# Layer 0's probabilities turned by VectorE and ordered through DRAM, and the norm sums of layer 1 moved to the next round

## The chip, the core and the metric

The kernel runs on one core of one Trainium2 chip. The metric is the device time of one execution in microseconds (us). Three executions of the kernel before took 3765.32, 3766.14 and 3766.64 us; the median is 3766.14.

## What is computed

x is 64 graphs of 256 nodes with 512 features, adj their 256x256 adjacency masks. Two pre-normed layers follow one another, each added to x. All is float32. Cut to what matters:

```python
h = jnp.maximum(_layernorm(x), 0.0)                       # layer 0
q, k, v = (split_heads(h @ W) for W in (Wq, Wk, Wv))      # 4 heads of 64
sim = jnp.einsum('bhid,bhjd->bhij', q, k) * scale
attn = jax.nn.softmax(jnp.where(adj, sim, neg), axis=-1)
x = x + merge_heads(jnp.einsum('bhij,bhjd->bhid', attn, v)) @ Wo + bo

h = jnp.maximum(_layernorm(x), 0.0)                       # layer 1, 8 heads of 64
m = h @ map_w.T + map_b
n = m_heads / jnp.maximum(norm(m_heads), COS_EPS)
cos_adj = (n @ n.T * ~adj) > THRESHOLD
q, k = m @ q_w.T + q_b, m @ k_w.T + k_b
p = softmax(where(adj, NEG, q @ k.T / sqrt(dk))) * keep
a = cos_adj * p
sem = h @ gcn_map_w.T + gcn_map_b
out = relu((a @ sem) @ gcn_W.T / (a.sum(-1) + 1.0))
x = x + out
```

## The kernel before

**Rounds.** One round handles two graphs at once: layer 1's attention of graph a (steps written as pairs, `("score", 2)`) and, of the next graph n = a + 1, layer 0 and the products of layer 1 that need only its features (steps written as strings, `"qk0"`). `rounds` (L271) writes the first round (n only, with weights still being folded), a loop over 62 rounds, one more round after the loop, and a last round (a only).

**Orders.** Each engine works through a hand-written list of steps in every round: TENSOR (L51), SCALAR (L58), VECTOR (L64), POOL (L73, GpSimd) and SYNC (L78, SyncE, which issues all DMAs of the rounds). An engine never leaves its order; a step waits at its head for semaphores of the others. So a wait holds up all that stands behind it on that engine.

**Precision.** Most products are made in three passes of fp32r (high x high, high x low, low x high; PASSES, L16). For that ScalarE writes the rounded high part of a result from PSUM to SBUF and VectorE then writes the low part, the difference. A product that needs this operand waits for both: PSUM, ScalarE, VectorE, TensorE. Matmuls with a transposed or a probability operand are plain float32.

**PSUM.** Banks 0 and 1 hold scores of layer 1 (a pair of heads), 2 and 3 cosines, 4 the values. All other products share banks 5, 6 and 7 in turn, in the order in which TENSOR lists them (`bank_of`, L86); `empty` (L912) makes TensorE wait until the bank's last user has been read out. When the list changes, so do the banks.

**Layer 0 of graph n.** ht0a, ht0b (L1026): eight TensorE transposes of h. qk0 to qk3 (L1031): q and k of two pairs of heads, 12 matmuls each. s0/s1 and s2/s3 (L1044): scores of a pair of heads, 12 matmuls of 64 rows with the two heads side by side. VectorE adds the mask and takes the row maximum (L811), ScalarE makes the exponential and the row sum (L629), VectorE the reciprocal ("sum", L818), GpSimd the scaling (L517). pt0 to pt3 (L1052): four TensorE transposes of 128x128 for each head, which ScalarE copies from PSUM to `ptm` (L636). av (L1057): probabilities times v0, 16 matmuls. wo0, wo1 (L1063); VectorE adds them to x_mid (L824) and takes the statistics, GpSimd the power for 1/deviation (`rstd_of`, L456), VectorE normalises ("norm1", L675). ht1a, ht1b: eight transposes, from which gT comes.

**Layer 1.** m0 to m3 (L1067) make m; ScalarE writes it to `m32` (L642), GpSimd its squares to `msq` (L524). `m32` and `msq` are the two halves of `ptm`: the buffer holds probabilities first and m afterwards. "ss" (L1085) sums the squares by head (16 small matmuls), VectorE clamps them (L846), "pow" on GpSimd makes the factor 1/norm (L547), "rt" (L1092) turns the factors, VectorE copies them in two parts (L848, L850), "bc0" and "bc1" (L1098) spread them over the partitions, VectorE multiplies m by them (L853). "unit" 0 and 1 then split the normed m into high and low: ScalarE L645, GpSimd L502 (semaphores nhigh_done and nlow_done). For each of four pairs of heads p: score p (L1006), cos p (L1011, which needs unit p // 2), on VectorE score_a/b (mask, L760), on ScalarE exp_a/b (L605), on VectorE cos_a/b (threshold and product, L771).

**How layer 1 turns its weights.** The 256x256 matrix of each head is to be transposed for the product with v. It is laid out in `att` in 32x32 blocks, so that one VectorE instruction ("flip", L779, 128x512) turns all blocks of a head in place. SyncE then writes the pair's 512 KB to `scratch` in DRAM ("spill", L390) and reads it back in four parts of 128 KB, one for each block column, into `uT` ("shift", L397), which puts the blocks in order. value p (L1015) uses it. `by_quarter` (L961) makes the score and cos products write their columns in this block order.

**The rest.** "back" p turns the values back, VectorE and GpSimd add them to x_res (L794, L510). "factor" p: three small VectorE operations. "mid" (L489): GpSimd adds bo to x. "mask0" (L481) and "mask1" make the masks. SYNC also has x (load), adj, out (store) and move (x_mid to x_res).

## Time and profile before

| | |
|---|---|
| median of three executions | 3766.14 us |
| the profiled execution | 3767.53 us |
| its span, first to last instruction | 3765.7 us |
| mean granted TensorE clock | 0.994 |
| busy: TensorE | 3665.0 us, 97% |
| busy: VectorE | 2723.6 us, 72% |
| busy: ScalarE | 1695.4 us, 45% |
| busy: GpSimd | 1357.2 us, 36% |
| DMA moved | 381.35 MB, 101 GB/s |

Busy time is the time in which at least one instruction of the engine ran; the shares are of the span. The sixteen DMA engines together are counted as one share. In a timeline or a chain the ends of TensorE's blocks overlap, so what a block takes is read from the start of the next one. "L949" is a line of the kernel; one helper line serves several steps, and the operands tell which. The chain of waits starts at the last instruction and goes back to what released each one; "issue" in it is time in which the engine waited for nothing that the profile shows.

### The profile page before, as it was taken

How to read it: one execution, taken by the hardware profiler on the slowest of the kernel's cores; microseconds unless marked ns; L12 is line 12 of the kernel's file. 1: busy time of each engine (PE TensorE's matmuls, PEld its weight loads, DVE VectorE, ACT ScalarE, POOL GpSimd, SP SyncE). 2: the span in 40 equal slices, each digit the busy share in tenths (PEclk: the TensorE clock that was granted, in tenths of full speed). 3: DMA queues.
4: the chain of work that ended last, by engine and by line, in shares of the span. 5: the costliest groups of instructions: out<-in, count | busy, mean ns of one | idle time of the engine just before them, and what ended most of it. 6: DMA issues, size and time to landing. Idle time of an engine off the chain costs nothing.

```text
span 3765.7 us, 101867 instructions
## 1 busy us (share of the span) xinstructions
PE 3665.0 (97%) x31020; PEld 3224.1 (86%) x31020; DVE 2723.6 (72%) x9432; ACT 1695.4 (45%) x5075; POOL 1357.2 (36%) x2069
## 2 busy tenths in 40 slices
PE   8999999999999999999999999999999999999997
PEld 5888888888888888888888888888888888888885
DVE  3777777777777777777777777777777777777765
ACT  2444444444444444444444444444444444444443
POOL 2333433433433333334334334334333333343331
PEclk9999999999999999999999999999999999999998
DMA  2223323233233233333232332322332333332323
GB/s 94 91 96 106 99 99 107 94 108 102 96 112 102 96 109 100 102 104 104 97 107 98 100 107 94 109 102 96 112 102 96 108 100 102 103 104 98 107 86 107
DMA packets 250601, 381.35 MB, mean 101 GB/s; under 512 B 41328, under 2 KB 173968, under 8 KB 250576
## 3 DMA queue, kind: packets, MB, share of 16 engines
q1 hardware_dynamic: 250304, 380.73, 30.4%
q0 software_dynamic: 272, 0.30, 0.0%
q8 instruction: 13, 0.21, 0.0%
q14 instruction: 12, 0.10, 0.0%
HBM read 179.61 MB, written 167.77 MB: 92 GB/s over the span
## 4 chain that ended last, share of the span: by engine, by line
PE 89%; DVE 5%; issue 4%; DMA 1%; DVEq 1%; POOL 0%; ACT 0%; SPq 0%; POOLq 0%; ACTq 0%
PE bank L949 35%; PE bank L957 19%; PE bank L973 14%; PE bank L981 8%; PE bank L942 7%; PE bank L1090 3%; DVE h L675 1%; DVE x_mid L824 1%; PE bank L1024 1%; PE bank L1102 1%; DVE rel L794 1%; PE bank L898 1%; PE bank L1096 1%; DVE mv L669 0%; DVE rec L785 0%
## 5 line engine op out<-in xcount | busy, mean ns | idle before, releaser
L605 ACT ACTIVATE att<-att,nmax 128x256 f32<-128x256 f32 x1024 | 508.1, 501 | 83.5 <-DVE nmax L760 83.5
L771 DVE SCALAR_TENSOR_TENSOR att<-bank,att 128x256 f32<-128x256 f32 x1024 | 404.9, 421 | 33.0 <-ACT att L605 18.3
L949 PE MATMUL bank<-gT,w_k 128*128 128x256 f32 x3072 | 417.2, 285 | 0.5 <-DVE k L841 0.5
L949 PE MATMUL bank<-gT,w_q 128*128 128x256 f32 x3072 | 414.6, 284 | 2.7 <-DVE w_k L698 1.4
L949 PEld LDWEIGHTS bank<-gT,w_map 128*128 128x128 f32 x3072 | 370.7, 188 | 34.3 <-issue 25.8
L949 PE MATMUL bank<-gT,w_map 128*128 128x256 f32 x3072 | 396.9, 285 | 1.1 <-DVE gT L801 1.1
L949 PE MATMUL bank<-hT,w_qkv 128*128 128x256 f32 x3072 | 392.6, 284 | 4.4 <-DVE hT L801 4.4
L949 PEld LDWEIGHTS bank<-gT,w_k 128*128 128x128 f32 x3072 | 386.7, 189 | 8.2 <-DVE k L841 0.7
L957 PE MATMUL bank<-w_v,gT 128*128 128x512 f32 x1536 | 385.2, 399 | 0.0
L949 PEld LDWEIGHTS bank<-hT,w_qkv 128*128 128x128 f32 x3072 | 373.2, 189 | 13.6 <-DVE w_o L689 4.8
L949 PEld LDWEIGHTS bank<-gT,w_q 128*128 128x128 f32 x3072 | 380.3, 189 | 3.7 <-DVE w_k L698 2.2
L760 DVE CUSTOM_DVE_ANT_0 att<-bank,mask 128x256 f32<-128x256 f32 x1024 | 378.8, 417 | 1.5 <-PE bank L973 1.5
L629 ACT ACTIVATE prob<-prob,nmax 128x256 f32<-128x256 f32 x512 | 255.2, 500 | 248.8 <-DVE nmax L811 248.8
L524 POOL TENSOR_TENSOR ptm<-ptm 128x256 f32<-128x256 f32 x256 | 157.5, 615 | 549.1 <-ACT ptm L642 546.9
L517 POOL TENSOR_SCALAR prob<-prob,rsum 128x256 f32<-128x256 f32 x512 | 242.4, 486 | 294.7 <-DVE rsum L818 294.7
L502 POOL TENSOR_TENSOR nrm<-ptm,nrm 128x512 fp32r<-128x512 f32 x128 | 166.1, 1298 | 486.0 <-ACT nrm L645 486.0
L779 DVE STREAM_TRANSPOSE att<-att 128x512 f32<-128x512 f32 x512 | 339.6, 692 | 0.0
L957 PEld LDWEIGHTS bank<-w_v,gT 128*128 128x128 f32 x1536 | 279.2, 188 | 58.6
L460 POOL TENSOR_SCALAR var_e<-mv 128x2 f32<-128x2 f32 x128 | 24.7, 193 | 755.7 <-DVE mv L669 750.1
L981 PE MATMUL bank<-uT,v 128*64 128x256 f32 x2048 | 276.2, 390 | 13.5 <-DMA uT<-scratch 13.5
L587 ACT ACTIVATE q<-bank,bias_q 128x256 fp32r<-128x256 f32 x128 | 60.8, 475 | 490.8 <-PE bank L949 490.8
L510 POOL TENSOR_TENSOR x_res<-x_res,rel 128x256 f32<-128x256 f32 x256 | 203.1, 793 | 198.9 <-DVE rel L794 198.9
(136 smaller groups left out, 7042.9 us busy)
## 6 DMA issues: line engine op xcount, KB each, us to landing
scratch<-att SPq DMA_DIRECT2D x256, 512.0 KB, 2.6
uT<-scratch SPq DMA_DIRECT2D x1024, 128.0 KB, 3.0
x_in<-x SPq DMA_DIRECT2D x64, 512.0 KB, 3.7
x_res<-x_mid SPq DMA_DIRECT2D x64, 512.0 KB, 2.9
out<-x_res SPq DMA_DIRECT2D x64, 512.0 KB, 2.8
adj<-adj SPq DMA_DIRECT2D x64, 64.0 KB, 1.9
att<-gcn_map SPq DMA_DIRECT2D x1, 1024.0 KB, 10.9
att<-map_rows SPq DMA_DIRECT2D x1, 1024.0 KB, 6.4
```

The costliest lines, as they stand in the source:

```text
L510: g.tensor_tensor(part, part, rel[:, :, :], ALU.add).then_inc(res_added, 1)
L517: last = g.tensor_scalar(prob0[:, hd, c, :], prob0[:, hd, c, :], rsum0[:, hd, c:c + 1], 0.0, ALU.mult, ALU.add)
L605: s_.activation(e_sl, e_sl, ACT.Exp, bias=nmax1[:, p, c, e:e + 1], scale=-1.0, accum_out=esum1[:, p, c, e:e + 1]).then_inc(exp1_done, 1)
L629: last = s_.activation(prob0[:, hd, c, :], prob0[:, hd, c, :], ACT.Exp, bias=nmax0[:, hd, c:c + 1], scale=-1.0, accum_out=esum0[:, hd, c:c ...
L760: v_.tensor_tensor_reduce(out=att[:, p % 2, :, e, c, :, :].rearrange("p b j f -> p b (j f)"), in0=in_blocks(score_bank[e][:, c * N:c * N + ...
L771: v_.scalar_tensor_tensor(e_sl, in_blocks(gram_bank[e][:, c * N:c * N + N]), COS_THRESHOLD, e_sl, ALU.is_gt, ALU.mult, accum_out=usum1[:, ...
L779: v_.transpose(blocks, blocks).then_inc(flipped, 1)
L942: last = t_.transpose(dst[:, b * 128:b * 128 + 128], src_of(outer, c), ident[:, :])
L949: last = t_.matmul(dst, w(ws, k)[:, t * 128:t * 128 + 128], rhs[:, rs, k, :], start=(k == 0 and i == 0), stop=(k == KT - 1 and i == 2))
L957: last = t_.matmul(dst, lhs[:, ls, k, c * 128:c * 128 + 128], w(ws, k), start=(k == 0 and i == 0), stop=(k == chunks - 1 and i == 2))
L973: last[e] = t_.matmul(order(banks[e][:, c * N:c * N + N], False), left[r, ls, c * 128:c * 128 + 128], order(right[r, rs, :], True), start= ...
L981: last = t_.matmul(dst[64 * e:64 * e + 64, :].rearrange("p (c r f) -> p c r f", c=C, f=32), v[:, jc, (hd0 + e) * DH:(hd0 + e + 1) * DH], r ...
```

## The change

1. **Turning.** `prob0` gets the block layout of `att`. The s products write in that order (`by_quarter`), mask0 is made in it (two GpSimd instructions of one row half each in place of one), and the operations of VectorE, ScalarE and GpSimd on the probabilities address it so. The steps pt0 to pt3 go, on TensorE and on ScalarE. In their place VectorE turns each head in place (turn0 to turn3, one 128x512 instruction each, after GpSimd's scaling), and SyncE writes each pair of heads to a new DRAM buffer `scratch0` (send0, send1) and reads it back in four parts into `ptm` (fetch0, fetch1). av waits for both pairs.
2. **Norm factors.** ss, pow, rt, bc0 and bc1 of a graph are no longer done at the end of the round that made m, but near the start of the next one, as ("ss", 0), ("pow", 0), ("rt", 0), ("bc", 0), ("bc", 1). So `m32` and `msq` live into that round, and the first fetch waits for nlow_done of both unit steps.
3. **Orders.** All five lists are written anew; with them the banks change. Among SyncE's steps the load of x stands between spill 3 and shift 3.

```diff
@@ the lists @@
     TENSOR = [
-        ("score", 0), "ht0a", "ht0b", ("k", 2), "qk0", "qk1", ("q", 2), ("cos", 0), "s0", "s1", ("score", 1), "qk2", "qk3",
-        ("vv", 0), "pt0", ("score", 2), ("cos", 1), "s2", "s3", "v0", "pt1", ("vv", 1), "pt2", "pt3", ("cos", 2), "av",
-        ("value", 0), ("cos", 3), "wo0", "wo1", ("k", 3), ("back", 0), ("q", 3), ("value", 1), "ht1a", "ht1b", ("back", 1),
-        ("score", 3), "m0", "m1", "m2", ("value", 2), "m3", "q0", ("back", 2), "ss", "q1", "k0", ("value", 3), "rt", "k1",
-        "bc0", "bc1", ("back", 3)
+        ("score", 0), "ht0a", "ht0b", ("ss", 0), "qk0", "qk1", ("rt", 0), "s0", "s1", "qk2", ("bc", 0), "qk3", ("bc", 1),
+        ("score", 1), "s2", "s3", ("cos", 0), ("k", 2), ("vv", 0), ("cos", 1), ("q", 2), ("vv", 1), "v0", ("cos", 2),
+        ("score", 2), ("value", 0), "av", ("q", 3), ("back", 0), "wo0", "wo1", ("k", 3), ("value", 1), ("score", 3),
+        ("back", 1), "ht1a", "ht1b", ("cos", 3), "m0", "q0", "m1", ("value", 2), "q1", "k0", "m2", ("back", 2), "k1",
+        ("value", 3), "m3", ("back", 3)
     ]
     SCALAR = [
+        "ht0a", "ht0b", ("exp_a", 0), "qk0", "qk1", ("exp_b", 0), "exp0", "qk2", ("unit", 0), "qk3", "exp1", "exp2", "exp3",
+        ("unit", 1), ("k", 2), ("q", 2), ("exp_a", 1), ("exp_b", 1), ("exp_a", 2), ("value", 0), ("exp_b", 2), "av", ("q", 3),
+        ("k", 3), ("value", 1), "ht1a", "ht1b", ("exp_a", 3), ("exp_b", 3), "m0", "q0", "m1", "q1", "k0", ("value", 2), "m2",
+        ("value", 3), "k1", "m3"
     ]
     VECTOR = [
+        ("score_a", 0), ("score_b", 0), "ht0a", "ht0b", ("ss", 0), "qk0", "qk1", ("rt", 0), "s0", "s1", ("bc", 0), "qk2",
+        "sum0", "qk3", ("bc", 1), "sum1", "turn0", "s2", "s3", "turn1", ("cos_a", 0), "sum2", ("cos_b", 0), "sum3",
+        ("flip_a", 0), ("flip_b", 0), ("k", 2), "turn2", "turn3", ("vv", 0), ("score_a", 1), ("q", 2), ("score_b", 1),
+        ("cos_a", 1), ("vv", 1), ("cos_b", 1), ("flip_a", 1), "v0", ("flip_b", 1), ("score_a", 2), ("score_b", 2),
+        ("cos_a", 2), ("factor", 0), ("factor", 1), ("flip_a", 2), "av", ("back", 0), ("cos_b", 2), ("q", 3), "wo0", "wo1",
+        ("flip_b", 2), ("k", 3), "norm1", ("score_a", 3), ("score_b", 3), "ht1a", "ht1b", ("factor", 2), ("cos_a", 3),
+        ("cos_b", 3), ("flip_a", 3), ("flip_b", 3), ("back", 1), ("factor", 3), "q0", "q1", ("back", 2), "stats0", "k0",
+        "norm0", "k1", ("back", 3)
     ]
     POOL = [
+        ("pow", 0), "mask0", "mid", ("unit", 0), "sum0", "sum1", "sum2", ("unit", 1), "sum3", "rstd1", ("back", 0), "mask1",
+        ("back", 1), "m0", "m1", "rstd0", ("back", 2), "m2", "m3", ("back", 3)
     ]
     SYNC = [
+        "send0", ("spill", 0), "fetch0", "send1", ("shift", 0), "fetch1", ("spill", 1), ("shift", 1), ("spill", 2),
+        ("shift", 2), ("spill", 3), "x", ("shift", 3), "adj", ("out", 0), "move"
     ]
@@ layout @@
-        prob0 = sb("prob0", [128, H0, C, N])
+        prob0 = sb("prob0", [128, PAIRS0, 4, 2, C, C, 32])
+        pT_blocks = [ptm[:, 2 * t:2 * t + 2, :].rearrange("p e n -> p (e n)").rearrange("p (r e c j f) -> p r e c j f", e=2, c=C, j=C, f=32)
+                     for t in range(PAIRS0)]
@@ SyncE @@
+                    elif kind in ("send0", "send1"):
+                        t = int(kind[4])
+                        sp.wait_ge(pturned, H0 * n + 2 * t + 2)
+                        if a is not None:
+                            sp.wait_ge(pT_in[t], 64 * n)
+                        sp.dma_start(scratch0[t, :, :, :, :], prob0[:, t, :, :, :, :, :].rearrange("p b e c j f -> p b e (c j f)")).then_inc(sent0[t], 16)
+                    elif kind in ("fetch0", "fetch1"):
+                        t = int(kind[5])
+                        sp.wait_ge(sent0[t], 16 * n + 32)
+                        sp.wait_ge(nlow_done, 2 * n + 2)
+                        for cols in range(4):
+                            sp.dma_start(pT_blocks[t][32 * cols:32 * cols + 32, :, :, :, :, :].rearrange("p r e c j f -> p r (e c j f)"),
+                                         scratch0[t, :, cols, :, :].rearrange("(r p) e x -> p r (e x)", p=32)).then_inc(pT_in[t], 16)
@@ VectorE @@
+                    elif kind in ("turn0", "turn1", "turn2", "turn3"):
+                        hd = int(kind[4])
+                        dve.wait_ge(prob0_done, H0 * n + hd + 1)
+                        blocks = prob0[:, hd // 2, :, hd % 2, :, :, :].rearrange("p b c j f -> p b (c j f)")
+                        v_.transpose(blocks, blocks).then_inc(pturned, 1)
@@ TensorE @@
-                        for last in head_products(pair_banks, qkm[:, :, t, :], qkm[:, :, 2 + t, :]):
+                        for last in head_products(pair_banks, qkm[:, :, t, :], qkm[:, :, 2 + t, :], by_quarter):
-                    elif kind[:2] == "pt":
-                        hd = int(kind[2])
-                        pe.wait_ge(prob0_done, H0 * n + hd + 1)
-                        empty(a, n, kind)
-                        transposes(full, lambda jc, c: prob0[:, hd, c, jc * 128:jc * 128 + 128]).then_inc(product_full, 1)
                     elif kind == "av":
-                        pe.wait_ge(pT_ready, H0 * n + H0)
+                        for t in range(PAIRS0):
+                            pe.wait_ge(pT_in[t], 64 * n + 64)
...
```

The steps ss, pow, rt and bc keep their instructions; only their place in the lists and their semaphores change. In the diff, waits of one engine are followed by a semaphore increment for bookkeeping, left out here.

## Rows read from the trace of the kernel before

**Rows 1.** The page: span, busy time by engine; costliest groups (busy us, mean ns); DMA issues (KB, us to landing)

```profile
span 3765.7 us, 101867 instructions
...
PE 3665.0 (97%) x31020; PEld 3224.1 (86%) x31020; DVE 2723.6 (72%) x9432; ACT 1695.4 (45%) x5075; POOL 1357.2 (36%) x2069
...
L779 DVE STREAM_TRANSPOSE att<-att 128x512 f32<-128x512 f32 x512 | 339.6, 692 | 0.0
...
uT<-scratch SPq DMA_DIRECT2D x1024, 128.0 KB, 3.0
```

**Rows 2.** TensorE's waits over the whole run: total us, times, longest

```profile
PE bank L942 <- DVE h L675: 61.1, 64, 8.4
```

**Rows 3.** Windows of a steady round and the last: length, busy us by engine, clock, DMA share, GB/s

```profile
1933.40:1990.60 57.20, 56.36 (x485) 49.86 (x484) 42.33 (x148) 26.25 (x79) 21.07 (x32) 1.00 0.30 102
...
3711.80:3765.70 53.90, 28.98 (x209) 20.98 (x208) 24.43 (x98) 12.79 (x42) 6.18 (x7) 0.76 0.32 108
```

**Rows 4.** Chain of waits, longest pieces: the same block, first and last of 62

```profile
106.07 5.67 PE bank L949 x48
...
3593.24 5.67 PE bank L949 x48
```

**Rows 5.** Chain of waits in one steady round: start us, us, what

```profile
1933.46 0.92 PE bank L973 x12
...
1941.07 2.34 PE bank L973 x36
...
1958.27 0.87 PE bank L942 x8
...
1971.51 0.12 issue
...
1982.56 1.68 PE bank L1090 x16
```

**Rows 6.** Timeline of TensorE: start us, us, line, operation

```profile
1906.47 3.06 PE L957 MATMUL bank<-w_o,oT 128*128 128x512 f32 x12
1909.37 1.58 PE L949 MATMUL bank<-gT,w_k 128*128 128x256 f32 x12
...
1930.96 0.38 PE L1096 MATMUL bank<-ident,rn 128*8 128x128 f32 x2
...
1936.65 3.00 PE L949 MATMUL bank<-hT,w_qkv 128*128 128x256 f32 x24
```

**Rows 7.** Timeline of VectorE: start us, us, line, operation

```profile
1911.00 0.41 DVE L669 BATCH_NORM_AGGREGATE mv<-stats 128x2 f32<-128x6 f32 x2
...
1927.12 0.17 DVE L846 TENSOR_SCALAR ssq<-bank 128x16 f32<-128x16 f32 x1 [0.91 <-PE bank L1090]
...
1931.83 0.41 DVE L850 TENSOR_TENSOR rnT<-bank,rnT 8x256 fp32r<-8x256 f32 x1
...
1940.11 0.43 DVE L805 TENSOR_TENSOR qkm<-bank,qkm 128x256 fp32r<-128x256 f32 x1 [1.00 <-ACT qkm L621]
```

**Rows 8.** Timeline of GpSimd: start us, us, line, operation

```profile
1911.98 0.71 POOL L463 TENSOR_TENSOR rstd<-var_e,minus_half 128x2 f32<-128x2 f32 x1 [0.18 <-POOL var_e L460]
...
1927.37 2.90 POOL L547 TENSOR_TENSOR rn<-ssq,minus_half 128x16 f32<-128x16 f32 x1 [1.23 <-DVE ssq L846]
```

**Rows 9.** Timeline of SyncE: a spill and its fetch undisturbed, then one beside the load of x

```profile
1912.35 0.34 SPq L396 DMA_DIRECT2D scratch<-att  x1
1915.16 1.73 SPq L404 DMA_DIRECT2D uT<-scratch  x4
...
1951.77 0.35 SPq L396 DMA_DIRECT2D scratch<-att  x1
...
1954.83 1.75 SPq L404 DMA_DIRECT2D uT<-scratch  x4
```

**Rows 10.** Windows: DMA share while one spill, then one fetch of 512 KB moves

```profile
1912.40:1915.20 2.80, 1.96 (x17) 1.30 (x16) 2.72 (x8) 1.23 (x3) 1.00 (x2) 1.00 0.46 187
1916.10:1919.50 3.40, 3.40 (x34) 3.26 (x33) 3.40 (x15) 2.19 (x9) 0.44 (x1) 1.00 0.58 154
```

More of the change, by code:

```diff
@@ L231, in gnn_two_layers @@
         high_done = count("high_done")
-        pT_ready = count("pT_ready")
+        pturned = count("pturned")
+        sent0 = [count(f"sent0_{t}") for t in range(PAIRS0)]
+        pT_in = [count(f"pT_in{t}") for t in range(PAIRS0)]
         m_ready = count("m_ready")
@@ L927, in empty @@
                 m = G - 1 if n is None else n - back
[L928 to L931 removed]
+                if user in MAPPED:
                     if a is not None or not back:
@@ L995, in body @@
                         full = bank[bank_of[s]]
-                    if kind in ("q", "k", "vv"):
+                    if kind == "ss":
+                        pe.wait_ge(msq_done, KT * a + KT)
+                        empty(a, n, s)
+                        for t in range(KT):
+                            for c in range(C):
+                                last = t_.matmul(full[:, c * H1 + 2 * t:c * H1 + 2 * t + 2], msq[:, t, c * 128:c * 128 + 128], half_of[:, :], start=True, stop=True)
+                        last.then_inc(later_full, 1)
+                    elif kind == "rt":
+                        pe.wait_ge(rn_done, a + 1)
+                        empty(a, n, s)
+                        for c in range(C):
+                            last = t_.transpose(full[0:H1, c * 128:c * 128 + 128], rn[:, c * H1:c * H1 + H1], ident[:, :])
+                        last.then_inc(later_full, 1)
+                    elif kind == "bc":
+                        pe.wait_ge(later_done, later_out_of_psum(a, ("rt", 0)))
+                        empty(a, n, s)
+                        for t in range(2):
+                            last = t_.matmul(full[:, t * N:t * N + N], pick[:, 2 * p + t, :], rnT[:, :], start=True, stop=True)
+                        last.then_inc(later_full, 1)
+                    elif kind in ("q", "k", "vv"):
                         pe.wait_ge(product_done, out_of_psum(a, "ht1b"))
```

104 lines of the change are left out of this document (40 added, 64 removed), and 4 rows, old and new, of the table SCALAR.

## The prediction

> **What bounds the kernel now.** I read the busy shares first: TensorE is busy 97% of the span, VectorE 72%, ScalarE 45%, GpSimd 36% [rows 1]. The reader is to see that one engine is nearly full. Then the waits: TensorE's one wait of size in the rounds is at the transposes of the second layernorm, 61.1 us in 64 times, all others being small or in the first and last rounds [rows 2]. The windows say the same of one round: TensorE idle 0.84 us of 57.2, at a granted clock of 1.00, VectorE busy 42.3 [rows 3]. The period comes from a block that the chain of waits shows once a round: (3593.24 - 106.07) / 61 = 57.17 us [rows 4]. So a steady round is 56.33 us of TensorE's work and 0.84 us of waiting, and there are 62 such in the loop and one after it. The last round is 53.9 us in which TensorE is busy 29.0, so there the chain of one graph sets the time [rows 3]. The profiled execution took 3767.5 us (span 3765.7), 1.4 above the median of the runs, 3766.1; my differences are added to the median.
>
> **What the change takes from TensorE.** Sixteen transposes of probabilities a round go. Eight take 0.87 us in the chain [rows 5], so sixteen take 1.75. The blocks of score, cos and s products pay for each uninterrupted run of them: a single one costs 0.92 and three in a row 2.34 [rows 5], which is 0.71 each and 0.2 per run. The old order has six runs and the new one seven, so 0.2 comes back. The reordered reading (by quarters) of the s products costs nothing: the score and cos blocks in the run of 2.34 already read so. ss, rt and bc are moved, not removed; each graph pays them once. New work: 56.33 - 1.75 + 0.20 = 54.78 us. Break-even is therefore 57.17 - 54.78 = 2.39 us of waits a round, where there were 0.84.
>
> A rule speaks against the change. The Trainium skill, VectorE: DVE Perf Modes, section Rules for kernel authors, says to use TensorE for a 128x128 transpose where PSUM can take the result, and that VectorE's transpose is the fastest only inside a bank of 32. By it the change would give up the right engine and buy a trip through DRAM; the rows give TensorE's side of the trade, 1.55 us a round before waits, and no row here shows the trip for layer 0.
>
> **What it puts on others.** VectorE gains four turns of a 128x512 tile, 0.65 each back to back (0.69 alone [rows 1]), 2.6 us, which makes 44.9 of 57: not the bound. ScalarE loses four evictions, GpSimd's mask becomes two instructions; neither is near full. DMA moves two more spills and two more fetches of 512 KB. One spill holds the engines 0.46 x 2.80 = 1.3 us, one fetch 0.58 x 3.40 = 2.0 [rows 10], so 6.6 us a round on a share of 0.30 (17 us) [rows 3]: about 0.42.
>
> **The new order, walked through.** t = 0 is the start of score 0.
> - Start: score, ht0, ss end at 0.92 + 0.87 + 1.68 = 3.5 [rows 5]; qk0 and qk1 follow, 2.84, to 6.3; rt could come and s0 at 6.45. But s0 needs the last eviction of qk1: in the trace qk0 starts at 1936.65 and VectorE ends the second copy at 1940.11 + 0.43, 3.89 later [rows 6, 7], and TensorE starts 0.12 after [rows 5]. Before, q2 and cos0 filled this; now only rt does. s0 starts at 7.5: **a wait of 1.05**. rt has its own wait, which lies inside: ssq is read after ht0b, at 3.9, GpSimd's power starts 0.25 later and takes 2.90 [rows 7, 8], so 7.1; it costs nothing while qk1's eviction is later.
> - qk2 then waits until rt is out of its bank (rt start to end of the second copy: 1931.83 + 0.41 - 1930.96 = 1.28 [rows 6, 7], so 8.4, plus 0.12) against 8.4 by work: 0.1 to 0.15; s2 waits about 0.1 for qk3. **0.2** together. cos0 needs bc0 (TensorE 10.2), VectorE's multiplication (11.1), unit 0 on ScalarE (11.7) and on GpSimd (13.05); TensorE gets there at 13.6. Behind the power wait on GpSimd stand mask0 (ready near 7.9, wanted at 8.6) and mid (wanted 27 us later): hidden, with 0.7 to spare for the mask.
> - The round trip. GpSimd scales head 0 only after unit 0, to 13.95; from there VectorE works almost without a break: turn0 to 14.65, s2 and s3 (0.7 each) to 16.05, turn1 16.7, cos 0 and both flips to 19.7, k2 20.1, turn2 20.75. turn3 waits for GpSimd, which does sum2, unit 1 and sum3 one after another to 20.7 (0.95, 1.3, 0.95), and ends at 21.45. SyncE issues in order: a spill is followed by its fetch 2.81 later (1912.35 to 1915.16), or 3.06 beside another transfer (1951.77 to 1954.83); the fourth part of a fetch is issued 1.3 into its 1.73 and lands 3.0 after that [rows 1, 9]. send1 goes out at 22.1, since fetch0 (which waits for unit1) fills the queue till then; 3.0 + 1.3 + 3.0 bring the second pair at 29.4, up to 30.3 with contention. TensorE, after value 0, wants it at 29.5. **0.3** taken (ends 0 and 0.8). shift 0, which now stands behind send1, lands at 27.5; value 0 wants it at 28.5. For this part TensorE does 21.7 us of work, so VectorE and the trip hide under it.
> - wo0 waits for VectorE's copy of av behind two factor steps and a flip, m0 for gT's behind four score steps: **0.2** together.
> - Layernorm of layer 1. Before, wo starts at 1906.47 and the mean and variance end at 1911.41, 4.94 later [rows 6, 7]; the power ends 1.28 after [rows 7, 8]; h needs 1.0 more. k3, back0, q3, value 1 stood between wo and ht1; now k3, value 1, score 3, back 1, 3.7 us in place of 4.25. score 3 waits for VectorE's copy of k3, behind the statistics and a flip: at 2.90 (wo, 1906.47 to 1909.37 [rows 6]) + 3.2 after wo's start; then ht1 waits a little for h. VectorE on its part drops a back and a factor step ahead of norm1. **0.85**, as much as the 0.84 before.
> - value 2 (data 0.7 early) and value 3 (0.1 to 0.4 early, with x's load now between spill 3 and shift 3): nothing, and this is where x's move can cost. The next ht0 finds h 0.5 early.
>
> Sum of waits: 1.05 + 0.2 + 0.3 + 0.2 + 0.85 = 2.6. Round: 54.78 + 2.6 = 57.4, 0.2 longer than 57.17. Over 63 rounds +13 us. The first round loses ss (1.68 [rows 5]), rt and bc (about 3 us with the wait for the power; its probabilities' trip is covered by the folding of weights that precedes av); the last one gets them with nothing beside them: score and ss 2.6, power 3.15, rt 1.3, bc0 with its multiplication and the unit steps 3 bring cos 0 at 10, where it stood at 6 behind score 0, k2 and q2; waits for later transfers hide part of the 4. I take -3 and +3, with ends -5 and +8 for their sum. Against the profiled execution's own time that is 3767.5 + 13 = 3780.5, against the median **3766.1 + 13 = 3779 us.** The waits I hold to 2.0 and 3.6, so rounds from 56.8 to 58.4.
>
> **Rivals.**
> - **A, the gates close early (faster).** My five waits are read from old neighbours. If the lead that VectorE gets while TensorE waits for s0 carries through, the trip, wo0, m0 and qk2 cost nothing and score 3 half: 1.05 + 0.45 = 1.5 to 2.0, a round of 56.5, 3766.1 - 0.65 x 63 = 3725. For: many gates meet within 0.1 to 0.3 in my walk. Against: s0's wait follows from two rows and has no cover.
> - **B, transfers collide (slower).** Between 19.9 and 29.4 spill 0, fetch0, send1, shift 0 and fetch1 need 2 x 1.3 + 3 x 2.0 = 8.6 us of the DMA engines [rows 10], nine tenths of that stretch. If each landing slips by 0.5, send1 and fetch1 bring av 1.0 later, and value 2 and value 3, past their slack, 0.3: 58.7 a round, 3766.1 + 1.5 x 63 = 3861; a third of it gives 3800. It decides where the second pair lands more than 0.3 after TensorE wants it at 29.5. For: 3.06 in place of 2.81 beside one other transfer [rows 9]. Against: that is a quarter of a microsecond only, and the share stays under 1. The Trainium skill, DMA: Bandwidth & Descriptors, section Latency and other measured facts, gives HBM's latency as 0.2 us on average and 2 at high load; by it B would be the case if such a stretch counts as high load, which no row here shows.
> - **C, all is hidden (faster).** Waits stay 0.84: 55.6 a round, 3665. Against: the s0 wait alone forbids it, unless the eviction of qk1 overlaps in a way that the rows don't show.
>
> **Numbers.** My own case (57.0 to 57.9 a round, 3755 to 3812) gets 0.43, of it 0.13 within 0.2% of 3766, 0.28 slower, 0.02 faster; A 0.29 (of it 0.02 within); C 0.07; B 0.21. 0.2%, 7.5 us, is about what a measurement of this kernel can tell from none. Faster 0.36, same 0.15, slower 0.49. My case's own range is 3755 to 3812; for 8 in 10, with A down to 3712 and the nearer half of B, I give 3712 to 3835.
>
> **What would show it.** Right: the block of 48 or its successor returns every 57.4 us; TensorE waits before the s products on VectorE's qkm copy (1.05 x 63 = 66 us) and before the k,q products on VectorE's k (about 45); prob transposes are gone. A: the period near 56.5, waits of TensorE of 1.8 or less. B: TensorE waits for a fetch from scratch0 by over 1 us a round, and transfers land later than 3.0. Wrong altogether: a wait on GpSimd's power or its sums, or VectorE as releaser at many small places.

## The result, and the profile after

The changed kernel takes 3973.58 us in the median (3973.0 to 3979.24), the kernel before 3766.24 beside it: ratio 1.0554, 95% interval 1.0536 to 1.0573. It is slower, by 207 us, far outside the range of the prediction (3712 to 3835).

The page of the changed kernel: span, busy times, and DMA issues with KB and us to landing.

```profile
span 3977.4 us, 100973 instructions
...
PE 3686.2 (93%) x29996; PEld 3148.7 (79%) x29996; DVE 2890.9 (73%) x9688; ACT 1578.3 (40%) x4819; POOL 1353.4 (34%) x2133
...
scratch<-prob SPq DMA_DIRECT2D x128, 512.0 KB, 3.1
ptm<-scratch SPq DMA_DIRECT2D x512, 128.0 KB, 3.2
```

Against [rows 1] TensorE has 1,024 instructions fewer, the transposes, and yet is busy 21 us longer. Its share fell from 97% to 93%: something else now holds it up. TensorE's waits of the changed kernel (total us, times, longest):

```profile
PE bank L1012 <- DMA ptm<-scratch: 87.8, 62, 2.0
PE bank L1004 <- DVE k L768: 47.1, 63, 0.8
PE bank L1038 <- POOL rn L577: 39.6, 64, 3.3
PE bank L1012 <- DMA uT<-scratch: 36.7, 74, 4.7
PE bank L973 <- DVE h L701: 28.4, 64, 8.4
```

Where there was one wait of size in the rounds [rows 2] there are five, and the greatest ends with a transfer from scratch0: av waits 1.4 us in every round of the loop. L768 is score 3 behind k3, L577 is rt behind GpSimd's power. The windows of one round, of two stretches of its round trip, and of the last round:

```profile
2022.82:2082.92 60.10, 56.33 (x467) 48.43 (x467) 44.90 (x152) 24.42 (x75) 21.00 (x33) 1.00 0.42 132
2062.50:2066.50 4.00, 4.00 (x30) 3.68 (x29) 3.97 (x17) 2.17 (x8) 0.00 (x0) 1.00 0.95 294
2066.50:2071.20 4.70, 3.18 (x37) 2.25 (x35) 3.59 (x16) 1.85 (x8) 0.00 (x0) 1.00 0.95 249
3919.70:3979.00 59.30, 34.21 (x218) 25.50 (x218) 25.31 (x99) 12.85 (x42) 8.94 (x8) 0.72 0.29 99
```

VectorE's 44.9 and the DMA share of 0.42 over a round are what was forecast against [rows 3]. But in the 8.7 us that end with av the DMA engines are busy 95% of the time. The same stretch in SyncE's timeline, and then in the chain of waits:

```profile
2056.88 0.35 SPq L401 DMA_DIRECT2D scratch<-prob  x1
2059.50 0.34 SPq L422 DMA_DIRECT2D scratch<-att  x1
2060.22 1.92 SPq L410 DMA_DIRECT2D ptm<-scratch  x4
2062.53 0.34 SPq L401 DMA_DIRECT2D scratch<-prob  x1
2063.15 2.09 SPq L430 DMA_DIRECT2D uT<-scratch  x4
2066.59 1.73 SPq L410 DMA_DIRECT2D ptm<-scratch  x4
```

```profile
2062.53 3.90 DMA scratch<-prob
...
2067.88 3.27 DMA ptm<-scratch
...
2071.48 1.95 PE bank L1012 x16
```

The second send (2062.53) takes 3.90 us to land where a lone spill and its fetch lay 2.81 apart [rows 9]; after it the fetch takes 1.3 to issue and 3.27 more. The chain now passes through this trip in every round: its shares are TensorE 29%, DMA 23%, issue 16%, VectorE 13%. Of the 23% only 11 are the trip (scratch<-prob 6, ptm<-scratch 5); 9 are the store and the move of x, which the chain reaches through GpSimd's "mid". But GpSimd stands idle after mid, as its timeline shows, and VectorE's under it:

```profile
2051.58 1.28 POOL L531 TENSOR_TENSOR nrm<-ptm,nrm 128x512 fp32r<-128x512 f32 x1 [1.08 <-ACT nrm L671]
```

```profile
2053.94 0.71 DVE L814 STREAM_TRANSPOSE prob<-prob 128x512 f32<-128x512 f32 x1 [0.71 <-POOL prob L547]
```

So mid is not what holds up the round. Unit 0 waits 1.08 us for its high part from ScalarE, which waits for VectorE's product behind bc0, and bc0 stands behind s0, s1 and qk2; head 0 is scaled only after unit 0, and turn0 waits 0.71 for that. The moved norm steps thus stand on the way from s0 to av. What they cost there no run shows, as none moves unit 0 alone.

**The granted clock.** It is 1.00 in the round above, but not in every round. In 15 of the 62 rounds of the loop it falls to 0.50, the lower of its two levels, for about 3.4 us. The fall comes within 0.5 us of av's start, after the two waits at value 0 and av. One such place, in two windows and TensorE's timeline:

```profile
1946.00:1949.60 3.60, 1.80 (x20) 1.02 (x19) 2.97 (x17) 2.14 (x8) 0.00 (x0) 1.00 0.97 276
1949.60:1953.00 3.40, 3.38 (x16) 1.90 (x16) 1.13 (x5) 0.20 (x2) 0.00 (x0) 0.50 0.34 95
```

```profile
1949.62 3.59 PE L1012 MATMUL bank<-ptm,v 128*64 128x256 f32 x16 [1.41 <-DMA ptm<-scratch]
```

av takes 3.5 us there in place of 1.9. A round with such a fall takes 61.9 us in the mean, one without 60.2. The kernel before has none in its loop.

**Where the 211.7 us between the two profiled spans went.** The norm sums ("ss") return once a round, so their starts measure it: 161.32 and, 61 rounds later, 3857.04, which is 60.58 a round, against 57.17 before. 62 rounds by 3.41 are +211. Some 3.0 of the 3.41 are longer rounds at full clock, 0.4 is the fallen clock (15 times 1.7 us). From the starts of score 0, the first round gives 5.0 back, the round after the loop takes 63.4 in both, and the last is 4.9 longer (58.8 against 53.9 [rows 3]). So everything is in the rounds of the loop, and the experiments are about those.

### The profile page after: what moved, and what is told of

It reads as the page before. It is cut to its first block, busy times and chain, and to the rows that moved or that the text cites. A ratio compares the mean times of both kernels' runs of the same rounds, so it can differ in the third digit from the quotient of the medians.

```text
span 3977.4 us, 100973 instructions
## 1 busy us (share of the span) xinstructions
PE 3686.2 (93%) x29996; PEld 3148.7 (79%) x29996; DVE 2890.9 (73%) x9688; ACT 1578.3 (40%) x4819; POOL 1353.4 (34%) x2133
## 4 chain that ended last, share of the span: by engine, by line
PE 29%; DMA 23%; issue 16%; DVE 13%; POOL 9%; SPq 6%; ACT 2%; DVEq 1%; POOLq 0%; ACTq 0%
PE bank L980 16%; DMA scratch<-prob 6%; PE bank L1012 5%; DMA ptm<-scratch 5%; PE bank L988 5%; SPq L410 5%; DMA x_res<-x_mid 5%; DMA out<-x_res 4%; POOL prob L547 2%; DVE h L701 2%; POOL x_mid L528 2%; DMA uT<-scratch 2%; DVE att L821 1%; DVE att L807 1%; DMA scratch<-att 1%
## 5 line engine op out<-in xcount | busy, mean ns | idle before, releaser
L980 PE MATMUL bank<-gT,w_map 128*128 128x256 f32 x3072 | 418.3, 285 | 12.9 <-DVE k L884 6.5
L980 PE MATMUL bank<-gT,w_q 128*128 128x256 f32 x3072 | 425.7, 288 | 1.4 <-DVE w_k L724 1.4
L980 PEld LDWEIGHTS bank<-gT,w_map 128*128 128x128 f32 x3072 | 379.8, 188 | 53.8 <-DVE k L884 34.7
L980 PE MATMUL bank<-hT,w_qkv 128*128 128x256 f32 x3072 | 413.5, 287 | 4.3 <-DVE hT L843 4.1
L807 DVE SCALAR_TENSOR_TENSOR att<-bank,att 128x256 f32<-128x256 f32 x1024 | 383.2, 416 | 3.4 <-PE bank L1004 3.2
L1004 PE MATMUL bank<-k,q 64*128 64x256 f32 x3072 | 245.6, 292 | 47.1 <-DVE k L768 47.1
L1004 PEld LDWEIGHTS bank<-k,q 64*128 64x128 f32 x3072 | 199.8, 186 | 95.7 <-issue 85.3
L847 DVE TENSOR_TENSOR qkm<-bank,qkm 128x256 fp32r<-128x256 f32 x256 | 108.1, 422 | 219.0 <-ACT qkm L651 219.0
L1004 PE MATMUL bank<-nrm 64*128 64x256 f32 x3072 | 247.2, 292 | 2.3 <-DVE att L807 1.6
```

The source lines that it names most:

```text
L807: v_.scalar_tensor_tensor(e_sl, in_blocks(gram_bank[e][:, c * N:c * N + N]), COS_THRESHOLD, e_sl, ALU.is_gt, ALU.mult, accum_out=usum1[:, ...
L847: v_.tensor_tensor(qkm[:, 1, 2 * w + t, :], full[:, 0:N], qkm[:, 0, 2 * w + t, :].bitcast(F32), ALU.subtract).then_inc(product_done, 1)
L980: last = t_.matmul(dst, w(ws, k)[:, t * 128:t * 128 + 128], rhs[:, rs, k, :], start=(k == 0 and i == 0), stop=(k == KT - 1 and i == 2))
L1004: last[e] = t_.matmul(order(banks[e][:, c * N:c * N + N], False), left[r, ls, c * 128:c * 128 + 128], order(right[r, rs, :], True), start= ...
```

## The experiments

In all of them the kernel changed is the base, unless the text says otherwise. The periods are read from the starts of "ss", as above.

**1. The trip left out.** SyncE's sends and fetches go, and av reads prob0 turned in place, so the ordering of the 32x32 blocks is left out.

```diff
-        "send0", ("spill", 0), "fetch0", "send1", ("shift", 0), "fetch1", ("spill", 1), ("shift", 1), ("spill", 2),
+        ("spill", 0), ("shift", 0), ("spill", 1), ("shift", 1), ("spill", 2),
@@ av @@
-                            last = values(full[:, t * N:t * N + N], v0, 2 * t, lambda e, jc: pT_blocks[t][:, :, e, :, jc, :]...
+                            last = values(full[:, t * N:t * N + N], v0, 2 * t, lambda e, jc: prob0[:, t, :, e, :, jc, :]...
```

> The changed kernel without layer 0's trip through DRAM: send0, send1, fetch0 and fetch1 are left out, av multiplies the turned blocks where they stand, out of order (the ordering of the blocks between 32-row groups is left out). All lists else as in the changed kernel. Theory T (the path of the second pair of heads, from turn3 through SyncE and DRAM to av, sets the round of 60.1 us): TensorE's waits before av (1.4 us) and value 0 (0.4) go and the round falls to 57.7 to 58.2, so about 3974 - 63 x 2.2 = 3835 us (3820 to 3855). Theory N (the moved norm steps with their waits before rt and s0 set it): TensorE is late at av anyway, the round stays over 59, 3900 or more.

Measured: 3838.76 us, ratio 1.0189 (1.016 to 1.0219), 58.30 a round. TensorE's timeline of this kernel at value 0 and av:

```profile
2051.80 1.08 PE L1012 MATMUL bank<-uT,v 128*64 128x256 f32 x8
2052.72 1.90 PE L1012 MATMUL bank<-prob,v 128*64 128x256 f32 x16
```

No wait stands between them. So the trip costs 60.58 - 58.30 = 2.28 us a round, 135 us in all. No round of the loop has a fallen clock here, so 0.4 of the 2.28 is the clock and 1.9 the waits. But this kernel, which pays nothing for ordering the blocks, is still slower than before: the trip is not the whole loss.

**2. The trip with a quarter of the bytes,** as many instructions on the same queue.

```diff
+                        part = 128 if a is None else 64
+                        heads = 2 if a is None else 1
+                        sp.dma_start(scratch0[t, :, :, 0:heads, 0:part], ...
+                            rows = 4 if a is None else 1
+                            sp.dma_start(pT_blocks[t][32 * cols:32 * cols + 32, 0:rows, ...
```

> The changed kernel with the same sixteen-odd instructions of the trip on SyncE, but after the first round each send and fetch moves only a quarter of its bytes (a quarter of the probabilities is ordered, the rest of ptm is left as it was). T by contention (the transfers stretch each other: the second send lands after 3.9 us where a spill alone took 2.6): landings fall to under 2.6, the wait before av goes, 3835 to 3870. T by queue (SyncE's order and the fixed part of a transfer): the data still come 1 us or more too late, 3900 to 3950. Theory N: no change, 3960 or more.

Measured: 3846.98 us, ratio 1.0211 (1.0181 to 1.0241), 58.4 a round; no wait at av. Of the 2.28 all but 0.1 goes with the bytes, and not with the instructions or the semaphores of the trip; the clock does not fall in the loop here either. The page's landings of this kernel:

```profile
scratch<-prob SPq DMA_DIRECT2D x126, 128.0 KB, 2.2
ptm<-scratch SPq DMA_DIRECT2D x504, 32.0 KB, 2.1
```

**3. Is it the neighbours' bytes or its own?** Layer 1's first pair, whose spill and shift run among the four new transfers, moves a quarter of its bytes (the rest of that pair's matrix is left out); layer 0's trip is whole. (One more load ahead of the loop costs 5.5 us.)

```diff
+                        heads, part = (1, 64) if p == 0 else (2, 128)
+                            rows = 1 if p == 0 else 4
```

> The changed kernel with layer 0's trip whole, but layer 1's first spill and its fetch (pair 0) moving only a quarter of their bytes by the same number of instructions (three quarters of that pair's turned matrix is left out; one more copy in DRAM at the start, some 3 us). Theory C (transfers that overlap stretch each other): fetch0 and send1 have less beside them, send1 lands after 3.0 to 3.3 instead of 3.9, the wait before value 0 goes and the one before av shrinks: 3974 - 63 x 1.2 + 3 = 3900 (3880 to 3925). If the landing is long because of its own bytes and of fetch0 alone: over 3940.

Measured: 3946.01 us, ratio 1.0477 (1.0447 to 1.0508). TensorE's waits of this kernel:

```profile
PE bank L1017 <- DMA ptm<-scratch: 98.0, 62, 2.4
```

value 0 no longer waits (8.7 us in the whole run) and the landings of the trip fall to 3.0 in the median. But the second send still takes 3.7 in the mean, against 3.9, and av still waits 1.6. The loss of 135 us falls by 28 (33 without the extra load), a quarter. That is the second expectation (over 3940). Of the gain 0.37 us a round is a shorter way to av; much of the rest is the clock, which falls in 2 rounds of the loop and not in 15. So the larger part goes with the trip's own bytes.

**4 and 5. The order on the queue.** send1 went out 1.0 us after turn3, behind fetch0. First it goes ahead of fetch0; then GpSimd also scales head 3 before unit 1.

```diff
-        "send0", ("spill", 0), "fetch0", "send1", ("shift", 0), "fetch1", ("spill", 1), ("shift", 1), ("spill", 2),
+        "send0", ("spill", 0), "send1", "fetch0", ("shift", 0), "fetch1", ("spill", 1), ("shift", 1), ("spill", 2),
@@ and in the second @@
-        ("pow", 0), "mask0", "mid", ("unit", 0), "sum0", "sum1", "sum2", ("unit", 1), "sum3", "rstd1", ("back", 0), "mask1",
+        ("pow", 0), "mask0", "mid", ("unit", 0), "sum0", "sum1", "sum2", "sum3", ("unit", 1), "rstd1", ("back", 0), "mask1",
```

> The changed kernel with send1 ahead of fetch0 on SyncE. In the changed kernel send1 was issued 1.1 us after turn3, behind fetch0's four parts, and landed 3.9 us later with fetch0 moving beside it. Theory Q+C (both the place in the queue and the collision count): send1 goes out 0.8 us earlier with one transfer fewer beside it, lands after 2.7 to 3.2, the second pair is there 1 us earlier but shift 0 a little later: the round loses 0.7 to 1.3 us, 3974 - 63 x 1.0 = 3911 (3890 to 3930). If only the number of bytes counts, whatever their order (theory C): within 20 us of 3974.

> As the run before, and on GpSimd sum3 ahead of unit 1, so that turn3 need not wait for unit 1's 1.3 us (turn3 ends 0.5 us earlier, fetch0 starts later). Theory T (the second pair's path sets the round): a further 0.3 to 0.8 us a round, 3860 to 3890, and not below the 3839 of the kernel without a trip.

Measured: 4083.24 us, ratio 1.0841 (1.081 to 1.0873), and 4028.71, ratio 1.0697 (1.0666 to 1.0728). Both are slower than the changed kernel; both expectations missed. The landings of the first, its waits, and its window over the three fetches:

```profile
scratch<-prob SPq DMA_DIRECT2D x128, 512.0 KB, 2.8
ptm<-scratch SPq DMA_DIRECT2D x512, 128.0 KB, 3.7
```

```profile
PE bank L1012 <- DMA uT<-scratch: 101.0, 71, 5.2
PE bank L1012 <- DMA ptm<-scratch: 88.3, 62, 1.6
```

```profile
2050.00:2060.40 10.40, 7.50 (x65) 6.21 (x63) 9.17 (x40) 4.62 (x17) 0.00 (x0) 1.00 1.03 249
```

The send lands sooner (2.8 in the median) and the fetches later (3.7): three fetches now run together, on DMA engines that are full (1.03). send1 is issued 0.8 us earlier, but fetch1 now stands behind all of fetch0 and shift 0 and is issued when it was before; its last part takes 4.4 us to land instead of 3.3, so the pair comes 1.0 later and value 0 is late as well. With that the clock falls in 30 of the 62 rounds, in 13 of them for 6.8 us: of the 110 us that this kernel loses on the changed one, about 60 are longer rounds at full clock (61.18 against 60.22) and much of the rest is the clock. The second kernel is 54.5 us better than the first. Its turn3 ends 0.63 us earlier after s0, and av starts 0.63 earlier: lateness on this way comes out one to one at av.

**6 and 7. The wait before s0.** Two kernels fill it. In the first, k2 stands between qk1 and rt on all three engines; in the second, score 1 stands before s0, on TensorE alone, which moves no bank.

```diff
-        ("score", 0), "ht0a", "ht0b", ("ss", 0), "qk0", "qk1", ("rt", 0), "s0", "s1", ...
+        ("score", 0), "ht0a", "ht0b", ("ss", 0), "qk0", "qk1", ("k", 2), ("rt", 0), "s0", "s1", ...
@@ the second @@
-        ..., ("rt", 0), "s0", "s1", "qk2", ("bc", 0), "qk3", ("bc", 1), ("score", 1), "s2", "s3",
+        ..., ("rt", 0), ("score", 1), "s0", "s1", "qk2", ("bc", 0), "qk3", ("bc", 1), "s2", "s3",
```

> The changed kernel with the step (k, 2) moved on TensorE, ScalarE and VectorE from behind cos 0 to between qk1 and rt, where TensorE waits 0.6 for rt and then for s0. Theory N: the cover takes 0.9 to 1.2 us out of every round, 3974 - 63 x 1.0 = 3910. Theory T: the waits at the front vanish and come back before av, since turn3 is not earlier: within 15 us of 3974.

> The changed kernel with one step of TensorE's list moved: score 1, 0.92 us, stands before s0 instead of behind bc1, and fills the 1.2 us that s0 waits for the eviction of qk1; no bank changes, as scores have their own. Everything is computed. Theory S (the waits of a round add up): 0.75 less a round, 3974 - 47 = 3927 (3910 to 3945). Theory P (a chain through the probabilities, from s0 over VectorE, GpSimd and the DRAM trip to av, sets the period; the wait before s0 costs nothing of its own and av waits by whatever the order gains): s0 comes no earlier, up to 0.1 later, av's wait stays near 1.6 plus what the order saved, 3970 to 3985.

Measured: 4067.29 us, ratio 1.0796 (1.0764 to 1.0827), and 4016.57, ratio 1.0661 (1.0643 to 1.0679). The first missed both numbers: with k2 moved, the banks shift, and the s products come to wait for k2's eviction (L768, 107.0 us in 127 times), so s0 starts 9.23 after score 0 instead of 7.76. That lateness of 1.47 came out one to one: the time rose by 93.7 us, 1.49 a round. The second kernel has no such side effect. Its timeline at rt, score 1, s0, and at av, with that of the changed kernel under it:

```profile
2064.16 0.38 PE L1038 MATMUL bank<-ident,rn 128*8 128x128 f32 x2 [0.58 <-POOL rn L577]
2064.48 0.99 PE L1004 MATMUL bank<-k,q 64*128 64x256 f32 x12
2065.30 0.88 PE L1004 MATMUL bank<-qkm 64*128 64x256 f32 x12
...
2070.68 0.98 PE L1004 MATMUL bank<-qkm 64*128 64x256 f32 x12 [0.88 <-DVE qkm L847]
...
2089.42 0.87 PE L1012 MATMUL bank<-ptm,v 128*64 128x256 f32 x6 [1.45 <-DMA ptm<-scratch]
```

```profile
2046.74 0.38 PE L1038 MATMUL bank<-ident,rn 128*8 128x128 f32 x2 [0.58 <-POOL rn L577]
2047.28 0.98 PE L1004 MATMUL bank<-qkm 64*128 64x256 f32 x12 [0.16 <-issue]
...
2052.74 0.98 PE L1004 MATMUL bank<-qkm 64*128 64x256 f32 x12
...
2071.48 1.30 PE L1012 MATMUL bank<-ptm,v 128*64 128x256 f32 x10 [1.44 <-DMA ptm<-scratch]
```

From rt to s0 it is 1.14 instead of 0.54, and from s0 to av 24.12 against 24.20: the same. s2, its cover gone, stands where it stood after s0 (5.38 and 5.46) and now shows a wait of 0.88. The 0.6 us by which s0 is later is the round's (43 us in all, 0.7 a round; 0.5 in the rounds at full clock). The waits do not add up (that theory expected 3927); the path from s0 over the softmax, the turns and the trip to av keeps its length, and TensorE's filling inside it buys nothing. The rival's mechanism holds; its number (3970 to 3985) was too low, as it allowed s0 0.1 us of lateness and not 0.6.

The means over the rounds of the loop show the same for all kernels so far. They are from TensorE's starts, in us; the first three columns are of rounds without a fall of the clock:

| | ss to s0 | s0 to av | av to the next ss | rounds with a fall, of 62 |
|---|---|---|---|---|
| the changed kernel | 5.92 | 24.30 | 30.00 | 15 |
| 1, no trip | 5.93 | 22.18 | 30.22 | 0 |
| 2, a quarter of the bytes | 5.93 | 22.21 | 30.30 | 0 |
| 3, neighbour lighter | 5.93 | 23.93 | 29.99 | 2 |
| 4, send1 first | 5.92 | 25.27 | 29.99 | 30 |
| 5, and sum3 earlier | 5.92 | 24.76 | 29.99 | 34 |
| 6, k2 early | 7.40 | 24.32 | 29.99 | 11 |
| 7, score 1 as cover | 6.52 | 24.16 | 30.01 | 16 |

In the rounds with a fall it is av to ss that is longer: 31.6 in the changed kernel, 32.0 in kernel 4.

**8. The turning alone, its lists half new.** The norm steps go back to the end of their own round, the trip stays.

```diff
-        ("score", 0), "ht0a", "ht0b", ("ss", 0), "qk0", "qk1", ("rt", 0), "s0", "s1", "qk2", ("bc", 0), "qk3", ("bc", 1),
+        ("score", 0), "ht0a", "ht0b", "qk0", "qk1", "s0", "s1", "qk2", "qk3",
...
-        ("value", 3), "m3", ("back", 3)
+        ("value", 3), "rt", "k1", "bc0", "bc1", ("back", 3)
```

> The turning by VectorE and the trip alone: ss, pow, rt and bc are back at the end of the round that made m, in the order that the kernel before has there; the lists else as in the changed kernel. Theory N: the round falls to about 57.5, 3800 us or less. Theory T: the trip is as long as before, but its start, s0, comes 2 us earlier after the start of the round (5.7 where it was 7.8) because ss and rt no longer stand ahead of it, while TensorE's work before av shrinks by as much, so the wait before av stays 1 us or more; the rest gains from the front's waits: 58.5 to 59.5 a round, 3880 to 3930.

Measured: 4257.43 us, ratio 1.13 (1.1268 to 1.1333). A miss that decides little: the lists written for it made new waits of their own (hT 104.5 us, qkm 75.3, rel 53.9), the mean granted clock was 0.97, and the wait at av stayed, 88.3.

**9. The norm steps and lists alone.** TensorE keeps the sixteen transposes (between q2 and cos 2, as the new order has room), no turns, no trip.

```diff
-        ("score", 1), "s2", "s3", ("cos", 0), ("k", 2), ("vv", 0), ("cos", 1), ("q", 2), ("vv", 1), "v0", ("cos", 2),
+        ("score", 1), "s2", "s3", ("cos", 0), ("k", 2), ("vv", 0), ("cos", 1), ("q", 2), "pt0", ("vv", 1), "pt1", "v0",
+        "pt2", "pt3", ("cos", 2),
```

> The other part alone: the norm steps in the next round and the new lists, but layer 0's probabilities transposed by TensorE and copied by ScalarE as in the kernel before (pt0 behind q2, pt1 behind vv1, pt2 and pt3 behind v0). Theory N (the moved norm steps and the new lists cost by themselves): the kernel without a trip took 58.3 us a round; sixteen transposes add 1.75, so 60.0 a round, 3838.8 + 110 = 3949 us (3925 to 3965), that is as slow as the whole change. If the turning and the trip are the only loss: 3766 to 3800.

Measured: 3985.16 us, ratio 1.0581 (1.055 to 1.0612), beyond the expectation. TensorE's waits of this kernel and its busy time:

```profile
PE bank L984 <- DVE k L754: 39.3, 63, 0.6
PE bank L984 <- DVE qkm L825: 27.8, 62, 0.9
PE bank L1018 <- POOL rn L558: 24.0, 50, 3.3
```

```profile
PE 3796.2 (95%) x31020; PEld 3259.2 (82%) x31020; DVE 2753.9 (69%) x9432; ACT 1702.2 (43%) x5075; POOL 1346.6 (34%) x2069
```

It runs the instructions of before, 31,020 on TensorE, in 219 us more, of which the busy time takes 131. Some 20 of these are 14 rounds of the loop in which the granted clock falls to 0.50 for 3.4 us, here at qk0 and qk1, and which take 61.7 us in place of 60.2. For the rest, a matmul's busy time in the profile includes a tail during which the next one may already start (the blocks of the timelines overlap by some 0.1 us), and short waits hide in it. Block starts against block starts, one round each: qk0 and qk1 take 3.50 where two such blocks took 2.84 before, rt to s0 0.70 (rt's work is 0.14), score 0 1.09 for 0.92, and so on.

**10. The other corner: old lists, no transposes.** The lists of before; the four pt steps give way to four turns on VectorE, no trip.

```diff
-        ("vv", 0), "pt0", ("score", 2), ("cos", 1), "s2", "s3", "v0", "pt1", ("vv", 1), "pt2", "pt3", ("cos", 2), "av",
+        ("vv", 0), ("score", 2), ("cos", 1), "s2", "s3", "v0", ("vv", 1), ("cos", 2), "av",
@@ VectorE @@
-        "sum2", ("cos_a", 1), ("factor", 0), "v0", "sum3", ("cos_b", 1), ("flip_a", 1), ("flip_b", 1), ("score_a", 2),
+        "sum2", ("cos_a", 1), "turn1", ("factor", 0), "v0", "sum3", "turn2", ("cos_b", 1), "turn3", ("flip_a", 1), ...
```

> The lists of before with only this exchanged: the four transposing steps of layer 0 leave TensorE and ScalarE, VectorE turns the four heads, the norm steps stay at the end of their round. The order of the 32x32 blocks is left out (no DRAM trip; av reads prob0 turned in place), so layer 0's values are not the reference's. With the runs so far this completes a two-by-two: old or new lists, with or without the sixteen transposes. Theory N (moving the norm steps with the lists written for it costs about 3.4 us a round, and the transposes are worth their 1.75): round 57.17 - 1.75 = 55.4, 3655 us (3645 to 3685). Theory L (the new lists are not the loss by themselves; what the norms-only kernel paid came of transposes that no longer fitted in the new order): the old lists without transposes gain little since GpSimd and VectorE gates close, 3740 or more.

Measured: 3791.28 us, ratio 1.0067 (1.005 to 1.0084), 57.68 a round. Theory N's 3655 is off by 136; theory L's number (3740 or more) is met, though it spoke of a small gain and this is a small loss. The greatest wait of this kernel, and its timeline from cos 2 to cos 3:

```profile
PE bank L1004 <- DVE att L798: 100.9, 126, 1.0
```

```profile
2026.90 0.99 PE L1004 MATMUL bank<-nrm 64*128 64x256 f32 x12 [0.63 <-DVE att L798]
2027.82 1.95 PE L1012 MATMUL bank<-prob,v 128*64 128x256 f32 x16
2030.00 1.08 PE L1012 MATMUL bank<-uT,v 128*64 128x256 f32 x8 [0.23 <-DVE v L755]
2032.06 0.98 PE L1004 MATMUL bank<-nrm 64*128 64x256 f32 x12 [0.98 <-DVE att L798]
```

Sixteen transposes, 1.84 us from start to start before, are gone. The rest of the round became 2.35 longer: cos 2 and cos 3 wait for VectorE to read the last cosines out of their banks (L798), which now stands behind the turns. The work went off TensorE, and the round did not get shorter: the next gate was VectorE's, and VectorE had received 2.6 us of work.

The four corners, in us (1, 9, 10 and the two kernels of the case):

| | transposes on TensorE | turned by VectorE, no trip | turned, with the trip |
|---|---|---|---|
| old lists, norms in place | 3766 | 3791 | 4631 |
| new lists, norms moved | 3985 | 3839 | 3974 |

The gain of the exchange depends on the lists: +25 us in the old ones, -146 in the new ones, where the rounds at full clock go from 60.22 to 58.33, by 1.89 and so by all that the transposes take; some 20 of the 146 are the clock. Theory L was right in this: the new lists cost 219 us with the transposes in them and 47 without.

**11 and 12. Old lists with the trip.** Kernel 10 with sends and fetches behind shift 0; then av also behind value 0 and cos 3.

```diff
-        ("spill", 0), "x", ("shift", 0), ("spill", 1), ("shift", 1), ...
+        ("spill", 0), "x", ("shift", 0), "send0", "fetch0", "send1", "fetch1", ("spill", 1), ("shift", 1), ...
@@ the second, TensorE @@
-        ("vv", 1), ("cos", 2), "av", ("value", 0), ("cos", 3), "wo0", "wo1",
+        ("vv", 1), ("cos", 2), ("value", 0), ("cos", 3), "av", "wo0", "wo1",
```

> The previous kernel but one (old lists, VectorE turns, norm steps in their old place) with the DRAM trip put in: sends and fetches of both pairs stand behind shift 0 on SyncE, av waits for both. Everything is computed. The old order has only vv1 and cos 2 between the last turn and av, where the changed kernel's trip took 10.0 us from the end of turn3 to av. Theory T (av is late by the trip less its cover): some 5 to 7 us of wait a round on 55.4, 3990 to 4120 us, and TensorE's wait for ptm from scratch0 is 300 to 450 us in all. Rival (the old order gives the turns early enough): av waits under 2 us a round, 3780 or less.

> As the kernel before it, with av behind value 0 and cos 3 in TensorE's list, 3.4 us of other work more between the last turn and av. Everything is computed. Theory T: 3.4 less wait a round unless value 0 becomes late behind the sends on SyncE's queue, so 150 to 210 us under the previous kernel, about 3850 (3790 to 3950). Rival (the four extra transfers make value 0 and others late by as much): within 60 us of the previous kernel.

Measured: 4630.79 us, ratio 1.2296 (1.2275 to 1.2316), and 4675.08, ratio 1.2414 (1.2393 to 1.2435). In the first, the kind of wait was as expected and its size twice that; in the second, the expected gain of 150 to 210 us did not come. Windows of one round of the first: up to cos 2, the wait for the trip, av, what follows:

```profile
2046.40:2059.40 13.00, 0.39 (x7) 0.18 (x4) 4.51 (x19) 2.19 (x8) 0.00 (x0) 0.68 0.62 201
2059.40:2064.00 4.60, 4.59 (x22) 2.73 (x24) 0.23 (x1) 0.60 (x1) 0.00 (x0) 0.50 0.00 0
2064.00:2070.00 6.00, 6.00 (x41) 4.61 (x38) 3.58 (x6) 0.39 (x1) 0.00 (x0) 0.95 0.35 87
```

TensorE's idle stretch is 12.6 us. Within it the granted clock falls to 0.50, and it stays there for the next 4.6 us, so av takes 3.46 us in place of 1.8. In the second kernel av starts at the same place as in the first (48.14 and 48.10 after q0), whatever stood before it. What the cover should have saved goes elsewhere: wo0 waits 1.4 for av's copy, which value 0 and cos 3 had covered, and then takes 4.4 us at the fallen clock in place of 2.9. The new lists leave 10 us between the last turn and av; in the old ones the trip costs 13 us a round, not 2.3. Of these 13, 4.5 are the order written for SyncE: turn3 ends at 2046.39, but send1 goes out at 2050.92, behind fetch0, which waits for the first send to land. No run tests another order there.

## Why the prediction was wrong

The sign of the likeliest case was right, its size was not: 3.41 us a round against 0.2. Slower had been given 0.49, so the sign is little to the forecast's credit.

- **The round trip: "0.3 taken (ends 0 and 0.8)" is the term that failed.** av and value 0 together wait 2.0 us from start to start in the round shown, 2.1 in the mean, and the clock that falls there takes 0.4 more. The second pair was to land at 29.4 after score 0 and av starts at 32.0, 2.6 later. Of that 0.9 came before the send: turn3 ends at 22.0 and not 21.45, and send1 goes out behind fetch0 at 23.0 and not 22.1. After it I put 3.0 + 1.3 + 3.0 from a trace in which one transfer runs at a time [rows 9], while my own count said nine tenths of the DMA engines' time; measured were 4.06 + 1.3 + 3.27, and 0.33 to av's start. Experiments 1 to 3 show it: 2.28 us a round is the trip, nearly all of it for its bytes.
- **Rival B named this mechanism** and its point of decision, and priced it at half: av 1.0 later, against 2.0 to 2.1 of waits. It expected value 2 and value 3 late as well. value 2 is not; k1 and value 3 are 0.3 to 0.5 us longer, where I had put nothing, but they are as long in experiment 1, without the trip (2.85 together, against 2.86), so this is not B's. The Trainium skill, DMA: Bandwidth & Descriptors, section Latency and other measured facts, has HBM's latency grow from 0.2 to 2 us at high load. The trace does not contradict it: the second send's 3.90, against 2.6 in the median of the spills without the trip, is a step of 1.3 inside that, though no run shows the latency by itself.
- **s0: 1.05 forecast, 1.2 measured,** but the reason was half another. rt waits 0.58 for GpSimd's power, and s0 starts behind it. I had named that as "wrong altogether"; it ties with the eviction of qk1 within a quarter of a microsecond.
- **Layernorm of layer 1: 0.85 forecast, 1.24 measured** (score 3 0.8, ht1 0.44). **qk2, s2: 0.2** against 0.15; **wo0, m0: 0.2** against 0.13.
- **Work: 54.78 forecast.** The round shown, 60.10, less the waits of 5.1 to 5.3 just listed is 54.8 to 55.0. The transposes' 1.75 is confirmed (1.84 before, from start to start).
- **The granted clock** has no term in the sum: it was 1.00 in the rounds of before. It takes 0.4 us a round.
- **First and last round: -3 and +3** against -5.0 and +4.9: each larger, the sum as forecast.
- **The sum itself was the wrong model.** I added waits where TensorE meets its gates, as if TensorE's work set the round and a shorter order could pull it in. Experiments 4 to 7 and 12 show that the path from s0 to av carries lateness one to one into av or the round and takes up whatever cover is put in it. On the gain's side the answer depends on the lists: in the old ones the 1.75 that I took off came back as 2.35 elsewhere (experiment 10), in the new ones without the trip it did not come back (1.89 less, 9 against 1). The Trainium skill's rule (VectorE: DVE Perf Modes, section Rules for kernel authors) says to use TensorE for a 128x128 transpose where PSUM can take the result. In the old lists the runs agree with it: VectorE's turns were 25 us slower even with the ordering left out. In the new ones they do not: turns and trip together, 3974, are no slower than TensorE's transposes, 3985, and the two intervals overlap.
- **What the change costs, by its parts.** The parts depend on the order in which they are taken. First the lists with the moved norm steps, then the turns, then the trip: +219, -146, +135 us. First the turns: +25, then the lists +47, then the trip +135. I had argued no loss from the lists apart from s0 and a few tenths. Which of the norm steps' places and of the rest of the reordering makes the lists' loss is not separated by any run; the only kernel that moved the norm steps back (8) brought waits of its own.
- **Rivals A and C** are out: no gate closed early.

No kernel here beats the one before.

## What to carry to other kernels

Taking work off the fullest engine shortens a round only if the next gate behind it moves too; before counting the gain, walk the longest path through the other engines and see whether it is shorter than the round by as much as you take away. A transfer on such a path is priced by the load of the DMA engines in its own stretch, not by the share over the round: 0.42 over the round hid 0.95 where it mattered. Look at the granted clock in every round and not in one: waits that come close together can bring it down in some rounds alone. And a wait before a step that starts such a path cannot be had back with filling that delays the step.

## What was not expected of the hardware

- Landing times move with load: a 512 KB send took 2.6 us in the median of the kernel before, 3.1 in the changed kernel, 3.90 in its fullest stretch (share 0.95); the fetches' parts 3.0, 3.2 and, three fetches together at a share of 1.03, 3.7. A quarter of the bytes took 2.2 and 2.1, so by my estimate about 2 us of a landing is not for its bytes.
- TensorE's busy time and its listed waits both miss short waits: experiment 9 gained 131 us of busy time with not one instruction more, some 20 of them by the clock. Starts against starts show the others.
- In experiment 11 TensorE's granted clock fell to 0.50 within 12.6 us of idleness and stayed there for 4.6 us of work. In the changed kernel two waits, 0.4 and 1.4 us, with 1.1 us of work between them were followed by a fall in 15 rounds of 62, and not in the others, though the way from s0 to av was as long in both (24.3). What decides between them stays open. A wait can thus be paid twice.
